# New step tables for the first unit and the last batch, a moved load, and a rearranged start of experts and combination

## The reference

```python
x = x + layernorm(attn(layernorm(x)))
    # c_kv, c_q: 512 -> 128; k, q = latent projection joined with a position part of 32 per head
    # softmax(q k^T / sqrt(32)) v, then W_O
h = layernorm(x)
    # routed: sigmoid scores, 2 of 4 groups, top 2 of 16 experts, weights normalised
    # expert: relu(h up)^2 down with 256 inside; shared: relu(h su)^2 sd with 1024 inside
x = x + layernorm(routed + shared)
```

## Time and profile before

| | us |
|---|---|
| runs of the kernel, median of 3 | 1584.65 (1578.47 to 1589.17) |
| profiled execution, its own time | 1584.75 |
| profiled execution, span of the trace | 1582.9 |
| TensorE busy | 1500.9 (95% of the span), 7006 matmuls |
| VectorE, ScalarE, GpSimd busy | 975.5, 783.9, 812.4 |

### The profile page before, as it was taken

How to read it: one execution, slowest core, us unless ns; L and a number is a source line. 1 busy time by engine, 2 the same in 40 slices (tenths; PEclk the granted TensorE clock), 3 DMA queues, 4 the chain that set the end, 5 groups by cost and what they waited for, 6 DMA issues and landing times.

```text
span 1582.9 us, 21759 instructions
## 1 busy us (share of the span) xinstructions
PE 1500.9 (95%) x7006; PEld 1021.7 (65%) x7006; DVE 975.5 (62%) x1871; ACT 783.9 (50%) x1417; POOL 812.4 (51%) x828
## 2 busy tenths in 40 slices
PE   5699999999999999999998999997999999979997
PEld 3365666656666566666564677785666666658886
DVE  3667677676767676767668437841333333349998
ACT  3255567466575665656647354430222222365554
POOL 1176697777786977769679440013222222043341
PEclk9699999999999999999999999998999999999999
DMA  5869579588595895967953333419977777686773
GB/s 132 139 93 144 90 119 213 73 180 147 89 200 88 147 196 84 176 122 114 236 79 99 133 133 102 158 29 291 293 215 216 218 216 214 224 319 215 232 244 101
DMA packets 162759, 257.76 MB, mean 163 GB/s; under 512 B 20084, under 2 KB 70132, under 8 KB 160596
## 3 DMA queue, kind: packets, MB, share of 16 engines
q1 hardware_dynamic: 144584, 205.12, 57.3%
q0 software_dynamic: 14064, 46.02, 9.9%
q10 hardware_dynamic: 4000, 5.24, 1.0%
HBM read 103.74 MB, written 58.46 MB: 102 GB/s over the span
## 4 chain that ended last, share of the span: by engine, by line
PE 71%; DMA 10%; issue 6%; DVE 4%; POOL 3%; ACT 3%; SPq 2%; another core or an unknown queue 1%; DVEq 0%; POOLq 0%; ACTq 0%
PE bank L113 12%; PE bank L784 8%; PE bank L807 8%; PE bank L716 8%; DMA a<-a 8%; PE bank L624 6%; PE bank L638 6%; PE bank L738 6%; PE bank L643 5%; PE bank L654 5%; POOL a L1597 2%; PE bank L663 2%; PE bank L796 1%; PE bank L581 1%; DMA f<-f 1%
## 5 line engine op out<-in xcount | busy, mean ns | idle before, releaser
L1597 POOL TENSOR_TENSOR a<-a 128x512 f32<-128x512 f32 x384 | 498.6, 1326 | 99.5 <-ACT a L1410 54.1
L1410 ACT ACTIVATE a<-bank 128x512 f32<-128x512 f32 x512 | 296.3, 597 | 258.1 <-PE bank L643 218.6
L917 DVE TENSOR_REDUCE a<-bank 128x1 f32<-128x512 f32 x512 | 321.8, 681 | 79.9 <-PE bank L624 79.2
L113 PE MATMUL bank<-a 128*128 128x512 f32 (+1 forms) x864 | 238.1, 397 | 2.7 <-DVE s L869 1.6
L638 PE MATMUL bank<-a 128*128 128x512 f32 x512 | 217.8, 425 | 5.2 <-ACT a L1410 5.1
L643 PE MATMUL bank<-a 68*128 68x512 f32 x512 | 204.0, 398 | 0.4 <-ACT a L1400 0.2
L624 PE MATMUL bank<-a 128*128 128x512 f32 x512 | 180.6, 424 | 24.4 <-DMA a<-a 20.3
L1665 POOL DMA_INDIRECT f<-h_scratch,f x79 | 76.3, 965 | 229.6 <-DMA f<-f 202.6
L113 PEld LDWEIGHTS bank<-a 128*128 128x128 f32 (+1 forms) x864 | 158.6, 186 | 49.0 <-issue 6.7
L738 PE MATMUL bank<-c 128*128 128x512 f32 x768 | 180.5, 394 | 8.4 <-ACT c L1466 7.4
L716 PE MATMUL bank<-c 128*128 128x512 f32 x768 | 177.5, 390 | 1.5 <-ACT c L1451 1.1
(11 more groups left out here) (187 smaller groups left out, 1776.7 us busy)
## 6 DMA issues: line engine op xcount, KB each, us to landing
a<-a SPq DMA_DIRECT2D x272, 256.0 KB, 9.7
f<-f SPq DMA_DIRECT2D x316, 64.0 KB
yp_scratch<-f SPq DMA_DIRECT2D x79, 256.0 KB
a<-in_L_attn_x SPq DMA_DIRECT2D x15, 1024.0 KB, 11.8
x_scratch<-a SPq DMA_DIRECT2D x8, 1024.0 KB, 4.6
h_scratch<-a SPq DMA_DIRECT2D x8, 1024.0 KB, 13.2
hT_scratch<-s SPq DMA_DIRECT2D x8, 1024.0 KB, 9.9
c<-hT_scratch SPq DMA_DIRECT2D x8, 1024.0 KB
```

Of the source, the lines that this page charges most:

```text
L113: t = e.matmul(out, a[n], b[n], start=n == 0 and m == 0, stop=n == len(ah) - 1 and m == 2)
L917: e.tensor_reduce(K.mx[:, i, j:j + 1], K.MX[n % 3][:], AX.X, ALU.max).then_inc(Z.max, 1)
L1410: e.activation(K.pt[:, n % NP, :], K.SC[n % 2][:], ACT.Exp, scale=SCALE).then_inc(Z.exp, 1)
L1597: e.tensor_tensor(K.acc[:, j, :], a, K.pt[:, n % NP, :], ALU.add).then_inc(Z.acc, 1)
```

## The change

It touches six places. No matmul is added or removed.

1. `STEP` and `FIRST_STEP` get other numbers, most of them different by one or two steps. `START_STEP` now also has `tops`, `rows`, `values`, `k` and `q` for unit 0 (`k` and `q` at step 0), and `LAST_STEP` is a second table for the four units of the last batch.
2. `("load", 1)` stands behind `half_order(1)`, so behind the copies of unit 1.
3. In `first_order`, `weights 2` stands ahead of the first `fetch`, `weights 3` behind all of them, and the `move`s at step 30. GpSimd's `store` is gone: ScalarE issues the store to HBM itself.
4. The transposed expert tile stands in `K.fso`, which the shared `up` reads last, so that the first `e turn` waits for `up`.
5. Five tiles are gathered ahead instead of eight, `next h` comes behind the third.
6. For the last eight tiles (`MIXED`), GpSimd weighs and sums the two gathered rows (`mix`), and VectorE adds once instead of twice. The last tile's sum reads TensorE's bank directly, and its `rescale` comes ahead of the `finish` of the tile before it.

```diff
+START_STEP = {"n": (13, 14, 15, 15, 16, 17, 24, 24, 25, 26), "turn": (30, 31, 34, 35),
+        "tops": (4, 6, 6, 8, 9, 10, 12, 13, 14, 14, 14, 15, 16, 16, 16, 16), "rows": 27, "values": (17, 23, 26), "k": 0, "q": 0}
...
-    out += [("qr", 0, 0), ("qr", 0, 1), ("load", 1)] + vs + half_order(1) + [("sel",), ("bias",), ("split w", "o")]
+    out += [("qr", 0, 0), ("qr", 0, 1)] + vs + half_order(1) + [("load", 1), ("sel",), ("bias",), ("split w", "o")]
...
-                        ("fetch", [("fetch", i) for i in range(4)] + [("weights", 2), ("weights", 3)]
-                         + [("move", i) for i in range(3)] + [("fetch", i) for i in range(4, 7)])):
+                        ("fetch", [("weights", 2)] + [("fetch", i) for i in range(4)] + [("move", i) for i in range(3)]
+                         + [("fetch", i) for i in range(4, 7)] + [("weights", 3)])):
...
+AHEAD = 5
+MIXED = TILES[-8:]
...
-    out = [("gather", n) for n in range(R)] + [("next h",)]
+    out = [("gather", n) for n in range(3)] + [("next h",)] + [("gather", n) for n in range(3, AHEAD)]
...
-                more.append(("gather", PLACE[t] + R))
+                more.append(("gather", n))
+            if n - 1 < NT and TILES[n - 1] in MIXED:
+                more.append(("mix", TILES[n - 1]))
...
-    return out + settle() + settle()
+    last = settle()
+    return out + last[-1:] + last[:-1] + settle()
...
-    K.hTt = K.faT[:, 3:5, :]
+    K.hTt = K.fso
...
-            w.wait_ge(Z.dn, 4 * FIRST)
+            w.wait_ge(Z.up, 8 * FIRST)
...
+            w.wait_ge(Z.mix, MIXED.index(t) + 1)
+            e.tensor_tensor(sh, K.DN[t % 2][:] if t == NT - 1 else sh, K.ya[:, z, :], ALU.add).then_inc(*csteps.next())
...
         e.copy(K.sq[:, i % 2, :], K.DN[n % 2][:]).then_inc(Z.so, 1)
+        w.wait_ge(Z.so, n + 1)
+        e.dma_start(K.shv[n], K.sq[:, i % 2, :]).then_inc(Z.sos[i % 2], 16)
...
+    def mix(t):
+        n = PLACE[t]
+        z = n % R
+        ya, yc = K.ya[:, z, :], K.yc[:, z, :]
+        w.wait_ge(Z.cg[z], 32 * (n // R + 1))
+        e.tensor_scalar(ya, ya, K.g1[:, t:t + 1], None, ALU.mult).then_inc(*chain.next())
+        e.tensor_scalar(yc, yc, K.g2[:, t:t + 1], None, ALU.mult).then_inc(*chain.next())
+        w.wait_ge(Z.root, chain.n)
+        e.tensor_tensor(ya, ya, yc, ALU.add).then_inc(Z.mix, 1)
```

More of the change, by code:

```diff
@@ L146 @@
 FIRST_STEP = {
[L147 to L153, removed]
[11 rows of a table removed]
-START_STEP = {"n": (0, 0, 0, 0, 0, 1, 2, 12, 12, 13), "turn": (14, 15, 23, 29)}
+        "rest": (1, 2, 2, 3, 1, 2, 2, 3, 3, 3, 5, 5, 7, 7, 5, 5, 8, 9, 4, 7, 10, 10, 11, 10, 9, 10, 10, 10, 10, 10, 10, 10, 11, 12),
+        "prepare": (18,),
+        "early": (12, 13, 14, 14, 14, 14, 16, 16, 16, 17, 18, 18, 19, 19, 19, 19, 20, 20, 20, 20, 23, 27, 31, 31, 35, 35),
+        "late": (22, 22, 22, 22, 22, 22, 22, 22, 22, 22, 22, 23, 23, 23, 23, 23, 23, 23, 23, 23, 24, 24, 24, 24, 24, 27, 28, 28, 28, 29, 29, 30, 34, 35),
+        "weights": (33,), "invert": (33, 33, 34, 34, 34, 35, 35, 35, 35),
+        "fetch": (16, 22, 24, 26, 30, 30, 30, 30, 30, 30, 34, 35)}
+STEP = {"split up": (5, 17, 21, 25, 26, 27, 39, 43), "split h": (41, 42, 44, 44), "last values0": 9, "total0": 8, "invert0": 7,
[11 rows of a table added]
+START_STEP = {"n": (13, 14, 15, 15, 16, 17, 24, 24, 25, 26), "turn": (30, 31, 34, 35),
+        "tops": (4, 6, 6, 8, 9, 10, 12, 13, 14, 14, 14, 15, 16, 16, 16, 16), "rows": 27, "values": (17, 23, 26), "k": 0, "q": 0}
+LAST_STEP = {"last values0": 9, "total0": 9, "invert0": 7, "divide0": 5, "round0": 10, "low0": 16, "k0": 3, "q0": 9,
[9 rows of a table added]
 def beside_order(u):
@@ L172, in beside_order, with due_at @@
     at = []
+    def due_at(u, name):
+        key = f"{name}{g}"
+        return LAST_STEP[key] if b == B - 1 and key in LAST_STEP else STEP[key]
     def put(name, items):
-        where = START_STEP[name] if u == 0 and name in START_STEP else STEP[f"{name}{g}"]
+        where = START_STEP[name] if u == 0 and name in START_STEP else due_at(u, name)
         at.extend(((32 * u + n, 1), x) for n, x in zip(where if isinstance(where, tuple) else [where] * len(items), items))
@@ L188, in beside_order @@
     if u + 1 < NU:
-        due = STEP[f"tops{g}"]
+        due = START_STEP["tops"] if u == 0 else due_at(u, "tops")
         for n in range(16):
@@ L348, in take @@
         added.append(4 * b + i)
-        return [("take", b, i), ("add", 4 * b + i)]
+        return [("take", b, i)] * (4 * b + i < NT - 1) + [("add", 4 * b + i)]
     for b in range(FIRST, B):
@@ L395, in __init__ @@
         self.su2_hi, self.sd2_hi = make("su2_high"), make("sd2_high")
+        self.mix = make("mix_done")
         self.cg, self.cin, self.cs = many("cg_in", R), many("cx_in", R), many("cs_out", R)
@@ L532, in choose_room @@
     K.ntv = tile([P, E])
+HOME = (6, 7, 3, 4, 0, 1, 2)
 def expert_room(K):
@@ L538, in expert_room @@
     K.hx = K.fhT[:, 0]
-    K.eyo = [K.faT[:, 6, :], K.faT[:, 7, :], K.fso[:, 0, :], K.fso[:, 1, :]] + [K.faT[:, k, :] for k in (0, 1, 2)]
-    K.hTt = K.faT[:, 3:5, :]
+    K.eyo = [K.faT[:, k, :] for k in HOME]
+    K.hTt = K.fso
     K.eaT = K.faT[:, 5, :].rearrange("p (z f) -> p z f", z=2)
@@ L962, in split_h @@
             w.wait_ge(Z.eT2, NTILE)
-            for n in (2, 3):
-                w.wait_ge(Z.yps[n], 16 * ((LAST - n) // 7 + 1))
         w.wait_ge(Z.h_hi, 4 * b + k + 1)
@@ L1268, in add @@
         sh = K.sh[:, z, :]
-        if t >= EARLY:
+        if t == NT - 1:
+            w.wait_ge(Z.dn, t + 1)
+            w.wait_ge(Z.cs[z], 16 * (n // R))
+        elif t >= EARLY:
             w.wait_ge(Z.so, t + 1)
@@ L1474, in up @@
             w.wait_ge(Z.ed, NTILE)
-            home = {6: 0, 7: 1, 0: 4, 1: 5, 2: 6}
-            if i in home:
-                w.wait_ge(Z.yps[home[i]], 16 * ((LAST - home[i]) // 7 + 1))
+            if i in HOME:
+                n7 = HOME.index(i)
+                w.wait_ge(Z.yps[n7], 16 * ((LAST - n7) // 7 + 1))
         if n >= 2:
@@ L1653, in choose @@
         early[0] += 1
-    def store(b, i):
-        w.wait_ge(Z.so, 4 * b + i + 1)
-        e.dma_start(K.shv[4 * b + i], K.sq[:, i % 2, :]).then_inc(Z.sos[i % 2], 16)
     def fetch(i):
@@ L1686, in gather @@
         e.indirect_dma_start(K.yc[:, z, :], None, K.yp_d, bass.IndirectOffsetOnAxis(K.sl2[:, t:t + 1], 0)).then_inc(Z.cg[z], 16)
-    stages = {"scores": scores, "divide": divide, "root": root, "residual": residual, "split down": split_down, "choose early": choose,
-              "store": store, "fetch": fetch, "weights": weights, "gather": gather}
+    def mix(t):
+        n = PLACE[t]
+        z = n % R
+        ya, yc = K.ya[:, z, :], K.yc[:, z, :]
+        w.wait_ge(Z.cg[z], 32 * (n // R + 1))
+        e.tensor_scalar(ya, ya, K.g1[:, t:t + 1], None, ALU.mult).then_inc(*chain.next())
+        e.tensor_scalar(yc, yc, K.g2[:, t:t + 1], None, ALU.mult).then_inc(*chain.next())
+        w.wait_ge(Z.root, chain.n)
+        e.tensor_tensor(ya, ya, yc, ALU.add).then_inc(Z.mix, 1)
+    stages = {"scores": scores, "divide": divide, "root": root, "residual": residual, "split down": split_down, "choose early": choose, "mix": mix,
+              "fetch": fetch, "weights": weights, "gather": gather}
     for name, *at in K.order:
```

12 lines of the change are left out of this document (7 added, 5 removed), and 31 rows, old and new, of tables (LAST_STEP, STEP).

## The result

The changed kernel takes 1598.63 us (median of 5 runs, 1595.64 to 1602.56), the kernel before 1584.93 (5 runs, 1578.47 to 1589.17): a ratio of 1.0077, 95% interval 1.0057 to 1.0096. The forecast was 1563.5, 1.3% faster; it is 0.8% slower, outside the range.

What follows compares the result with a forecast made beforehand. TensorE was taken as full in the long stages, with some 45 us to win in four places and the tail. Terms of -5.5, -1, -2, 0, -6.1, -5, 0, -1.7 sum to -21.3: 1584.75 to 1563.5 us, range 1549 to 1579.

Steps and rivals of the forecast that it cites:

- Start of attention: Units 0 and 1: unit 1's tops start 7.0 us earlier as copies join the queue sooner; -5.5 us (bounds -2.5, -7).
- Middle tables: Attention's middle 26 units: steps move by one or two, with 7.0 us idle in all; -1 us (bounds -5, +5).
- Last batch: Attention's last batch: loss of 9.5 us idle and 3 us of clock, partly the same; -2 us (bounds -7, +3).
- First stage: Shared expert stage: weights and routing have slack before they are read; 0 us (bounds -2, +2).
- First expert tiles: First expert tiles: ideal gain -11.8 us, less 4 idle and 1.7 half clock; -6.1 us (bounds -11.8, +5).
- tile 3 arrives near 1096: First expert tiles: tile 3's move lands behind weights near 1096, `e up` 3 due at 1092.3; 4 us idle.
- Start of the combination: Combination's first batch: 10.4 us hang on a stall in a burst of 12.96 MB; -5 us (bounds 0, -8.3).
- Five gathers instead of eight take 2.4 MB out of it: Start of the combination: fewer gathers cut the 12.96 MB burst by 2.4 MB, 18%.
- Mix: Last eight tiles: GpSimd's additions slow VectorE's two-input additions; about +12 us, 1575.5 us in all; chance 0.05.
- TensorE bounds: 0: Combination: `mix` takes GpSimd 4 us beside a tile of 5.4, saves VectorE 0.79; 0 us.
- Tail: After the last matmul: one addition from the bank saves 1.4 us, reordering 0.3; -1.7 us (bounds -1, -2).
- Rival tables: Attention: new step tables make every unit wait; at 1 us a unit 1590.5 us; chance 0.05.

Runs made afterwards that it cites:

- e14: The kernel before, with the gathers of tiles 3 to 7 waiting for the last `up` of batch 4, on chip C: 1581.07 us, ratio 0.9953 to before.
- e1: The changed kernel, with SyncE issuing weight group 1 ahead of the first moves again: 1585.98 us, ratio 1.0005 to the kernel before.
- e2: The changed kernel, with the routing entry `"rest"` of `FIRST_STEP` from the kernel before: 1596.97 us, ratio 1.0071 to the kernel before.
- e4: The changed kernel, with GpSimd's gathers of tiles 3 to 7 waiting for the last `up` of batch 4: 1592.49 us, ratio 1.0044 to the kernel before.
- e13: The kernel before, unchanged, run again with a profile on chip C: 1589.15 us, ratio 1.0008 to before.

## Why the prediction was wrong

Between the sum's -21.3 and the profile's +17.8 lie 39.1 us: 9.6 in the first expert tiles, 7.9 at the start of the combination, 6.1 in its last three batches (`mix`), 5.1 in the first stage, 4.1 in the last batch, 3.0 in units 0 and 1, 1.8 ahead of unit 0, 1.4 in the tail and 0.1 in the middle. No one step explains the miss; each is taken in turn.

**Start of attention: right in kind, half in size.** The tops of unit 1 came at 67.92, which is the sum's 66 and the 1.8 us by which this execution reached unit 0 later (56.9 to 60.2 over all profiles, with either start, so mostly chance). Unit 0 became 4.6 us shorter. The step that failed is the term of -5.5, which ended at unit 1: half of batch 1's transposes, with their copies and splits, moved out of unit 0 and stand in unit 1 now, which grew by 2.1 us and got 3.4 us of half clock. From unit 0's first scores to unit 2's the new start took 53.6 to 55.7 us in fourteen profiles, 55.0 in the middle, and the old one 57.2 to 57.3 in three of four (60.2 in e14): -2.3.

**Middle tables: right** (-0.9 against -1; 664.3 to 665.3 with the new `STEP` in twelve profiles, 665.7 to 666.3 with the old in six).

**Last batch: wrong sign.** Idle time did fall, from 9.5 to 8.2 us, as the term of -2 had it; but TensorE's busy time rose from 93.3 to 96.7 us, and 10.2 us of half clock stand where 6.8 stood. The new table took 103.9 to 107.3 us in its ten profiles, the old entries 102.8 to 104.6 in eight. The step that failed took the clock as "partly the same" as the idle time, and so priced neither the clock nor the busy time by itself. How much of its growth is the clock's is open: e1, at full clock through the whole stage, has 95.0 us busy and took 103.9.

**First stage: the step "weights and routing have slack before they are read: 0" failed.** It looked at routing's readers alone and not at what stands behind its root on GpSimd: the casts. +4.2 in batch 0, of which e2 took back 3.5, and +0.9 in batches 1 to 3, which no run looked into.

**First expert tiles: the mechanism right, one term a third of its size.** The ideal of 8.0 us was met to 0.2 as soon as e1 took the obstacle away, and the obstacle was the one named: the move of tile 3 behind group 1 in SyncE's queue. I took 4 us for it and 1.7 for the clock; it was 12.2 us of idle time and about 3 of clock (13.7 us at half, in which TensorE worked 5.8). The step that failed is "tile 3 arrives near 1096": it let groups 1 and 3 land by 1090, as if they had the DMA engines from 1074 on to themselves. Group 1 was issued only at 1080.6 to 1086.4, since SyncE spent 8 us on the three moves ahead of it, and from 1082 to 1110 the queues of the changed kernel moved 9.8 MB, of which SyncE's queue, with group 1 and tile 3's move behind it, had 4.2:

```profile
q1 hardware_dynamic: 4612, 4.16, 49.1%
q10 hardware_dynamic: 2026, 2.87, 31.4%
q0 software_dynamic: 774, 2.71, 25.0%
```

ScalarE's queue (q10, late weights and two stores) had 2.9 MB, which the sum named and did not count. Nor does the early start keep all of its gain of 12 us: in the ten profiles with group 1 ahead, tiles 4 to 14 take 41.4 to 43.9 us, in the other eight 40.3.

**Start of the combination: wrong.** The step that failed is "Five gathers instead of eight take 2.4 MB out of it": it did not happen on GpSimd at all (e4). That the burst is behind the stall, as was suspected, the wait shows: with it the first batch takes 47.4 to 50.7 us from its first `up` to the next batch's, without it 55.5 to 60.1 on chips A and C and in the first two profiles, but for e1 (48.6). The changed kernel's +2.9 is within the scatter of that event: the kernel before took 55.6 us in its first profile and 59.5 in e13.

**Mix: the rival with a chance of 0.05 came true, at half of its price.** It cost 6.1 us in the windows of the last three batches, not 12. The step that failed is "TensorE bounds: 0", which priced `mix` at 4 us of GpSimd a tile and at nothing for VectorE; its three operations took 4.9 us (1.65, 1.79 and 1.44), and VectorE's stretched beside them until TensorE waited for ScalarE's relus behind them (3.1 us in the last batch). The argument against it, that VectorE's other operations did not stretch beside GpSimd, was about operations with one input from on-chip memory; the small products of the layer norm's scaling have two, and four of them stand in each tile's chain. The Trainium skill (SBUF — State Buffer, section "Who interferes with whom") has a VectorE instruction with two SBUF inputs contend with a GpSimd instruction that reads SBUF. The trace agrees, 0.92 us against 0.69 for L1343.

**Tail: the compute gain was right, and given back.** From the last matmul to VectorE's last addition the changed kernel takes 1.5 us less, but the last store was confirmed 3.7 us after it, in all four kernels with `mix` (the changed one, e1, e2, e4), and 2.5 in all others; why is open. The step that failed is the end of the path: the sum stopped at the issue of the last store and took its landing as fixed.

**Rival tables** (each unit waits) did not occur. What the forecast lacked was the sum over small risks: it gave 0.04 to slower, although four of its terms had an upper bound above zero; three of these ended above zero, the first stage 3 us beyond its bound, and the combination's two terms, whose upper bound was zero, ended at +2.9 and +6.1.
